# Second attention of a two-layer transformer block: probabilities and operands split and transposed in another way

## The reference, cut to what matters

```python
def second_attention(x, ctx, Wq, Wk, Wv, Wo, q_norm_w, k_norm_w, pos_ctx, pos_x):
    y = layernorm(x)                                   # per batch 128 x 256
    q = rms_norm(y @ Wq.T, q_norm_w)                   # 16 heads of 128
    kv_in = concatenate([ctx, y], axis=1)              # 256 keys
    k = rms_norm(kv_in @ Wk.T, k_norm_w)               # 4 key heads of 128
    v = kv_in @ Wv.T
    q, k = rope(q, pos_x), rope(k, [pos_ctx, pos_x])   # x*cos + rotate_half(x)*sin
    scores = q @ k.T / sqrt(128)                       # each key head serves 4 query heads
    attn = softmax(scores) @ v
    return attn @ Wo.T                                 # 2048 -> 256
```

## Time and profile before

| | us |
|---|---|
| median of 3 runs (949.36 to 957.8) | 949.4 |
| the profiled execution's own time | 950.05 |
| its span, first to last instruction | 948.3 |
| first to last keys-and-values matmul of the second attention | 311.8 to 820.1 |
| last output addition of the second attention | 864.4 |

### The profile page before, as it was taken

How to read it: one execution, slowest core, us unless ns; L and a number is a source line. 1 busy time by engine, 2 the same in 40 slices (tenths; PEclk the granted TensorE clock), 3 DMA queues, 4 the chain that set the end, 5 groups by cost and what they waited for, 6 DMA issues and landing times.

```text
span 948.3 us, 19290 instructions
## 1 busy us (share of the span) xinstructions
PE 786.5 (83%) x5555; PEld 525.6 (55%) x5555; DVE 817.4 (86%) x2370; ACT 599.3 (63%) x1452; POOL 597.1 (63%) x987
## 2 busy tenths in 40 slices
PE   0185989884675679999999999999999999984776
PEld 0152333331233457777777777777777777653433
DVE  7765789976895689999999999999999999954996
ACT  1565787762894267666667766666677766662552
POOL 1500111122573699999999999999999999841453
PEclk9995999997996899999999999999999999998997
DMA  8204355441254000000000000000000000000245
GB/s 302 100 1 135 110 159 158 148 132 49 55 96 94 24 23 7 29 9 22 30 28 2 29 29 23 8 29 30 2 29 29 29 1 13 12 12 12 43 101 120
DMA packets 89306, 53.72 MB, mean 57 GB/s; under 512 B 43988, under 2 KB 88438, under 8 KB 88950
## 3 DMA queue, kind: packets, MB, share of 16 engines
q1 hardware_dynamic: 89206, 52.54, 19.5%
HBM read 22.10 MB, written 6.29 MB: 30 GB/s over the span
## 4 chain that ended last, share of the span: by engine, by line
PE 59%; DVE 13%; issue 10%; POOL 7%; ACT 5%; DMA 3%; SPq 1%; POOLq 1%; DVEq 0%; ACTq 0%
PE psum L1590 8%; PE psum L1614 8%; PE psum L1558 8%; PE psum L1602 8%; PE psum L1545 7%; PE psum L1570 3%; PE psum L1580 3%; PE psum L515 3%; PE psum L1511 2%; DMA arena<-arena 2%; PE psum L501 2%; ACT arena L812 1%; ACT arena L806 1%; PE psum L1530 1%; DVE arena L830 1%
## 5 line engine op out<-in xcount | busy, mean ns | idle before, releaser
L1302 ACT ACTIVATE arena<-psum,arena 128x256 f32<-128x256 f32 x256 | 147.0, 589 | 2.8 <-DVE arena L1495 2.8
L1286 POOL TENSOR_SCALAR arena<-arena 128x256 f32<-128x256 f32 x256 | 123.4, 482 | 35.4 <-DVE arena L1456 13.0
L1311 ACT ACTIVATE arena<-psum 128x512 f16<-128x512 f32 x64 | 38.2, 597 | 158.8 <-PE psum L1614 158.8
L1558 PE MATMUL psum<-wq_t,arena 128*128 128x512 f16 x384 | 94.5, 383 | 4.5 <-DVE arena L1385 4.3
L1590 PE MATMUL psum<-wo_t,arena 128*128 128x256 f16 x768 | 94.4, 273 | 3.0 <-DVE arena L1396 3.0
L1602 PE MATMUL psum<-arena 128*128 128x256 f16 x768 | 94.3, 273 | 2.7 <-ACT arena L1302 2.7
L1545 PE MATMUL psum<-wkv_t,arena 128*128 128x256 f16 x768 | 95.6, 275 | 0.9 <-DVE arena L1422 0.9
L1614 PE MATMUL psum<-arena 128*128 128x512 f16 x384 | 93.3, 379 | 0.0
L1243 POOL TENSOR_TENSOR arena<-arena,minus_half 128x6 f32<-128x6 f32 x64 | 85.1, 1329 | 10.7 <-DVE arena L1487 6.9
L1251 POOL TENSOR_TENSOR arena<-arena 128x256 f32<-128x256 f32 x128 | 90.4, 727 | 0.3 <-DVE arena L1385 0.3
L343 POOL TENSOR_TENSOR arena<-arena 128x256 f32<-128x256 f32 x16 | 11.9, 745 | 116.9 <-DVE arena L422 116.9
(11 more groups left out here) (201 smaller groups left out, 2011.2 us busy)
## 6 DMA issues: line engine op xcount, KB each, us to landing
arena<-split_scratch SPq DMA_DIRECT2D x96, 64.0 KB, 2.6
arena<-in_x SPq DMA_DIRECT2D x32, 128.0 KB, 2.2
split_scratch<-arena SPq DMA_DIRECT2D x32, 128.0 KB, 1.8
x_rows<-arena SPq DMA_DIRECT2D x32, 128.0 KB, 2.0
arena<-x_rows SPq DMA_DIRECT2D x32, 128.0 KB, 2.1
arena<-in_L_ffn_w SPq DMA_DIRECT2D x2, 1024.0 KB, 6.8
x_rows<-in_L_xattn_Wq SPq DMA_DIRECT2D x1, 2048.0 KB, 13.3
ctx_t<-in_L_xattn_Wo SPq DMA_DIRECT2D x1, 2048.0 KB, 11.7
```

The lines of the kernel that those rows point to most:

```text
L1286: eng.tensor_scalar(probs[:, t, h, :], probs[:, t, h, :], share[:, t, h:h + 1], P_SCALE, ALU.mult, ALU.mult).then_inc(S["probs"], 1)
L1302: eng.activation(probs[:, t, h, :], S_BANKS[:, h, :], ACT.Exp, bias=bias[:, t, h:h + 1], scale=r[:, w.lane % 4, h:h + 1], accum_out=total[ ...
L1558: mm = eng.matmul(Q_BANK, y_t[:, p, s, k, :], c.wq_t[:, m, k, SHARE * P * g:SHARE * P * g + SHARE * P], start=(n == 0), stop=(n == 5))
```

## The change

The second attention is written anew, still with 64 units and one list per engine. The lags are now: rows 1, halves of y 2, transpose of y 3, projection 3, transpose of queries and keys 5, scores 6, high halves of the probabilities (PROBS) 7, low halves (LOWS) 8, values 9, output 10.

- No transpose is left on TensorE. SP issues three transposing DMAs per unit: 12 blocks for queries and keys, 8 for the high and 8 for the low halves of the probabilities. Each batch has one more, of 4 blocks, for `y`.
- Exponentials are written back into the score banks in PSUM, which are doubled. ACT makes the high halves from there with the scale `share`, DVE the low halves.
- Sums of squares come from ACT's Square with accumulation, and the inverse roots from its Ln and Exp in place of GpSimd's `pow`.
- DVE forms cosine and sine products in one instruction for the queries and one for each of the two key blocks.
- GpSimd adds the rotated parts, and makes the high and low halves of `y`, queries and keys. It no longer touches the probabilities.
- Rows, context and tables are read where they lie, with no copying DMA.

The diff, cut to its core (`unit(s, LAG)` is the unit of that stage in step s, or None; `batch` the same for the first unit of a batch):

```diff
-            for h in heads:
-                eng.activation(probs[:, t, h, :], S_BANKS[:, h, :], ACT.Exp, bias=bias[:, t, h:h + 1],
-                               scale=r[:, w.lane % 4, h:h + 1], accum_out=total[:, t, h:h + 1])\
-                   .then_inc(S["exps"], 1)
...
+    ROWS, HALVES, Y_TURN, PROJ, QK_TURN, SCORE, PROBS, LOWS, ATTEND, OUT = 1, 2, 3, 4, 5, 6, 7, 8, 9, 10
...
     def sync(eng):
+        def probs_turn(u, half):
+            eng.dma_start_transpose(p_t[:, u % 2, half, :, :, :].rearrange("p h k r -> p (h k) r"),
+                                    p_hl[:, u % 2, half, :, :].rearrange("p h k -> p (h k)"))\
+               .then_inc(p_turned[u % 2], 16)
+        for s in range(STEPS):
+            u = unit(s, LOWS)
+            if u is not None:
+                eng.wait_ge(S["p_lo"], u + 1)
+                probs_turn(u, 1)
+            u = unit(s, QK_TURN)
+            if u is not None:
+                eng.wait_ge(S["q_lo"], u + 1)
+                wait(eng, S["scores"], u - 1)
+                eng.dma_start_transpose(qk_t[:, u % 2, :, :], qk_hl[:, u % 2, :]).then_inc(qk_turned[u % 2], 16)
+            b = batch(s, Y_TURN)
+            if b is not None:
+                eng.wait_ge(S["y_lo"], b + 1)
+                wait(eng, S["q"], GROUPS * (b - 1))
+                eng.dma_start_transpose(y_t[:, b % 2, :, :, :].rearrange("p s k r -> p (s k) r"),
+                                        y_hl[:, :, :].rearrange("p s n -> p (s n)")).then_inc(y_turned[b % 2], 16)
+            u = unit(s, PROBS)
+            if u is not None:
+                eng.wait_ge(S["p_hi"], u + 1)
+                wait(eng, S["attn"], u - 1)
+                probs_turn(u, 0)
     def pool(eng):
...
+        for s in range(STEPS):
+            u = unit(s, PROJ)
+            if u is not None:
+                eng.wait_ge(S["k_cs"], u + 1)
+                wait(eng, S["k_lo"], u)
+                eng.tensor_tensor(straight(k_rot[:, :, :]), straight(k_cs[:, 0, :, :]), swapped(k_cs[:, 1, :, :]),
+                                  ALU.add).then_inc(S["k_rot"], 1)
...
+                wait(eng, qk_turned[u % 2], 16 * (u // 2))
+                eng.tensor_copy(k_hl(u, 0), flat(k_rot[:, :, :])).then_inc(S["k_hi"], 1)
...
+                eng.tensor_tensor(k_hl(u, 1), flat(k_rot[:, :, :]), k_hl(u, 0), ALU.subtract).then_inc(S["k_lo"], 1)
...
+            if u is not None:
+                eng.wait_ge(S["q_cs"], u + 1)
+                wait(eng, S["q_lo"], u)
+                eng.tensor_tensor(straight(q_rot[:, :, :]), straight(q_cs[:, 0, :, :]), swapped(q_cs[:, 1, :, :]),
...
+                eng.tensor_copy(q_hl(u, 0), flat(q_rot[:, :, :])).then_inc(S["q_hi"], 1)
...
+                eng.tensor_tensor(q_hl(u, 1), flat(q_rot[:, :, :]), q_hl(u, 0), ALU.subtract).then_inc(S["q_lo"], 1)
     def scalar(eng):
...
+        for s in range(STEPS):
+            u = unit(s, PROJ)
+            if u is not None:
+                eng.wait_ge(S["kv"], u + 1)
+                wait(eng, S["ss_k"], u)
+                wait(eng, S["r"], 2 * (u - 1))
                 for n in range(2):
+                    last = eng.activation(junk[:, SHARE + n, :], kv_view[:, n, 0, :], ACT.Square,
+                                          accum_out=sums[:, u % 2, SHARE + n:SHARE + n + 1])
+                last.then_inc(S["ss_k"], 1)
...
+                eng.activation(v[:, u % 8, 0, :, :], kv_view[:, :, 1, :], ACT.Copy).then_inc(S["v_hi"], 1)
+            u = s - PROJ
+            if 0 <= u <= TOTAL:
+                cols = slice(0 if u else SHARE, SHARE + 2 if u < TOTAL else SHARE)
+                eng.wait_ge(S["ss_k"], min(u + 1, TOTAL))
+                wait(eng, S["ss_q"], u)
+                wait(eng, S["r"], 2 * u)
+                eng.activation(log_ms[:, cols], sums[:, u % 2, cols], ACT.Ln, scale=1.0 / HEAD_DIM, bias=eps[:, 1:2])\
+                   .then_inc(S["r"], 1)
...
+                eng.activation(r[:, u % 8, cols], log_ms[:, cols], ACT.Exp, scale=-0.5).then_inc(S["r"], 1)
+            u = unit(s, PROBS)
+            if u is not None:
+                eng.wait_ge(S["share"], 2 * (u + 1))
+                eng.wait_ge(S["exps"], u + 1)
+                wait(eng, p_turned[u % 2], 32 * (u // 2))
+                for h in range(SHARE):
+                    last = eng.activation(p_hl[:, u % 2, 0, h, :], s_banks(u)[:, h, :], ACT.Copy,
+                                          scale=share[:, u % 2, h:h + 1])
+                last.then_inc(S["p_hi"], 1)
...
+            u = unit(s, PROJ)
+            if u is not None:
+                wait(eng, S["ss_q"], u)
+                wait(eng, S["r"], 2 * u)
+                eng.wait_ge(S["q_cs"], u + 1)
+                for h in range(SHARE):
+                    last = eng.activation(junk[:, h, :], Q_BANK[:, P * h:P * h + P], ACT.Square,
+                                          accum_out=sums[:, (u + 1) % 2, h:h + 1])
+                last.then_inc(S["ss_q"], 1)
+            u = unit(s, ATTEND)
+            if u is not None:
+                eng.wait_ge(S["attn"], u + 1)
+                wait(eng, S["o"], u - 1)
+                eng.activation(a_t[:, u % 2, 0, :], A_BANK, ACT.Copy, scale=A_SCALE).then_inc(S["a_hi"], 1)
+            u = unit(s, SCORE)
...
+                eng.wait_ge(S["bias"], u + 1)
...
+                for h in range(SHARE):
+                    last = eng.activation(s_banks(u)[:, h, :], s_banks(u)[:, h, :], ACT.Exp,
+                                          bias=bias[:, u % 2, h:h + 1], scale=r_q(u)[:, h:h + 1],
+                                          accum_out=total[:, u % 2, h:h + 1])
+                last.then_inc(S["exps"], 1)
     def vector(eng):
+        for s in range(STEPS + 1):
+            u = unit(s, LOWS)
+            if u is not None:
+                eng.wait_ge(S["p_hi"], u + 1)
+                for h in range(SHARE):
+                    last = eng.scalar_tensor_tensor(p_hl[:, u % 2, 1, h, :], s_banks(u)[:, h, :],
+                                                    share[:, u % 2, h:h + 1], p_hl[:, u % 2, 0, h, :],
+                                                    ALU.mult, ALU.subtract)
+                last.then_inc(S["p_lo"], 1)
...
+            if u is not None:
+                eng.wait_ge(S["a_hi"], u + 1)
+                eng.scalar_tensor_tensor(a_t[:, u % 2, 1, :], A_BANK, A_SCALE, a_t[:, u % 2, 0, :], ALU.mult,
+                                         ALU.subtract).then_inc(S["a_lo"], 1)
+            u = unit(s, PROBS)
+            if u is not None:
+                eng.wait_ge(S["exps"], u + 1)
+                eng.tensor_scalar(part[:, u % 2, :], total[:, u % 2, :], 1.0 / P_SCALE, None, ALU.mult)\
+                   .then_inc(S["share"], 1)
...
+            if u is not None:
+                eng.wait_ge(S["share"], 2 * u + 1)
+                eng.reciprocal(share[:, u % 2, :], part[:, u % 2, :]).then_inc(S["share"], 1)
...
+            u = unit(s, PROJ)
+            if u is not None:
+                bu = u // GROUPS
+                eng.wait_ge(S["r"], 2 * (u + 1))
+                eng.wait_ge(S["v_hi"], u + 1)
+                eng.wait_ge(S["tables"], bu + 1)
+                wait(eng, S["k_rot"], u)
+                for n in range(2):
+                    last = eng.scalar_tensor_tensor(
+                        k_cs[:, :, n, :], kv_view[:, n, 0, :].unsqueeze(1).broadcast_to([P, 2, HEAD_DIM]), r_k(u, n),
+                        turn["k"][:, bu % 2, :, n, :], ALU.mult, ALU.mult)
+                last.then_inc(S["k_cs"], 1)
+                eng.tensor_tensor(v[:, u % 8, 1, :, :], kv_view[:, :, 1, :], v[:, u % 8, 0, :, :], ALU.subtract)\
+                   .then_inc(S["v_lo"], 1)
...
+            if u is not None:
+                eng.wait_ge(S["q"], u + 1)
+                wait(eng, S["q_rot"], u)
+                eng.tensor_tensor(
+                    q_cs[:, :, :, :],
+                    Q_BANK.rearrange("p (h d) -> p h d", h=SHARE).unsqueeze(1).broadcast_to([P, 2, SHARE, HEAD_DIM]),
+                    turn["q"][:, bu % 2, :, :].unsqueeze(2).broadcast_to([P, 2, SHARE, HEAD_DIM]), ALU.mult)\
+                   .then_inc(S["q_cs"], 1)
+            b = batch(s, ROWS)
+            if b is not None:
+                eng.wait_ge(S["rstd"], 2 * (b + 1))
+                wait(eng, S["y_lo"], b)
+                eng.tensor_scalar(y[:, :], c.x_rows[:, b, :], mv[:, 0:1], rstd[:, :], ALU.subtract, ALU.mult)\
                    .then_inc(S["y"], 1)
+            u = unit(s, SCORE)
+            if u is not None:
+                eng.wait_ge(S["scores"], u + 1)
+                wait(eng, S["bias"], u - 1)
+                eng.tensor_reduce(top[:, u % 2, :], s_banks(u), AX.X, ALU.max).then_inc(S["top"], 1)
...
+                eng.scalar_tensor_tensor(bias[:, u % 2, :], top[:, u % 2, :], -1.0, r_q(u), ALU.mult, ALU.mult)\
...
     def tensor(eng):
+        for s in range(STEPS):
+            u = unit(s, PROJ)
+            if u is not None:
```

(46 more changed lines are left out.)

525 lines of the change are left out of this document (111 added, 414 removed).

## The result

The changed kernel takes **927.5 us** (median of 4, 921.53 to 938.8), the kernel before 952.9 beside it: ratio 0.9709, 95% interval 0.9626 to 0.9793. All ratios here compare the means of the fast runs, so this one leaves the run of 938.8 out as a slow one. The forecast was 995 with a chance of 0.19 for a time under 940, so it was wrong in sign. Where a stretch from the start is needed I take e7's profile, a kernel whose batches last as long (32.1 us).

What follows compares the result with a forecast made beforehand. TensorE was taken to set the pace at 8.22 us a step, ScalarE afterwards at 7.57. From 950.05: +56 (late `y`'s 92 included), -8 and -2 give 996, less 0.6 for the median 995 us; 8 in 10 range 930 to 1050.

Steps and rivals of the forecast that it cites:

- SP issues that transpose in the same step, third in its list: Each batch's first projection step: `y`'s transpose queues behind low halves, queries and keys, so the keys come late.
- a late `y`: Keys of the new rows wait for transposed `y`: 6.6 us a batch in 14 batches, 92 us.
- Rival A: SP's wait for the low halves ends some 6 us sooner, so `y` is not late: 903 us, chance 0.12.
- The ring: Waits between ScalarE and VectorE within one second-attention step, from key squares to exponentials, set the pace: 7.57 us.
- 0.24 us to spare: VectorE's maximum and bias run beside ScalarE's query squares and high half (1.73 us) and end 0.24 us sooner.
- beside the rest: GpSimd's new work, 6.2 us a step, lies beside the other engines' work as long as a step is longer.
- Two thirds of TensorE's saving is lost: Second attention: ScalarE becomes the pace, a batch takes 30.6 us against 32.9; TensorE alone would save 107 us.
- B: TensorE stays the pace at 6.55 us a step, ScalarE's waits hidden, `y` late: 934 us, chance 0.06.
- C: ScalarE's squares and copies at their lower ends, 7.0 us a step: 961 us, down to 944, chance 0.12.
- E: ScalarE's Square, Ln, Exp and Copy would reload the tables; nearly excluded, chance 0.01.
- D: Half clock through scores and values after each gap, or dearer squares: 1037 us and above, chance 0.14.
- a sign of error: Heads of the batches: no idle TensorE there would show the forecast wrong; it expected 6 us or more idle.

Runs made afterwards that it cites:

- e7: The changed kernel with SP issuing the transpose of `y` at the head of its step's list; 925.62 us.
- e1: The changed kernel with the transpose of `y` issued one step later, in the step of its own projection; 1030.61 us.
- e12: e2 with one query square instead of four (the other sums a constant) and the maximum over half of the keys; 900.03 us.
- e11: e2 with the maximum of the scores taken over half of the keys only; 909.5 us.
- e10: e2 with one query square instead of four on ScalarE, the three sums left out being a constant; 910.07 us.
- e2: The changed kernel with GpSimd's tables instruction moved behind the queries' halves; 907.72 us.
- e3: The changed kernel with the bias formed head by head, by four VectorE operations with one SBUF tensor and a pointer each; 918.31 us.
- e13: e12 with the bias formed head by head as in e3; 893.73 us.
- e9: e2 with the third pass left out of the queries' and output projections, 0.98 us a step less TensorE work; 910.15 us.

## Why the prediction was wrong

**The step that failed: "SP issues that transpose in the same step, third in its list".** The list of lags has ten names and ten numbers; the transpose of `y` is 3 and the projection is 4. I paired the projection with 3, the value that it had before, and the text on the change says so too ("projection 3"); the line of the diff is right. The transpose stands one step earlier in SP's list than its projection in TensorE's. In the window shown it is issued at 602.19, as TensorE comes to that projection; the matmuls on `y` run from 605.59 to 606.42, and ScalarE, still busy with squares and exponentials, wants the keys only at 607.48. In e1 it is issued at 544.47, when ScalarE has been done for 2 us. The 92 us of a late `y`, the largest correction in the sum, were charged to a wait that the change does not have. Rival A, "`y` is not late", was the true case; I named another place for it (SP's wait for the low halves), and gave it 0.12.

**What a late `y` would cost: nearly right.** I said 6.6 us a batch, half clock included; in e1 ScalarE's wait for the keys alone is 6.6, 15 times and not 14, and a batch lasts 39.2 us instead of 32.0, so 7.2. A transpose of 4 blocks landed after 2.9 us (median), where I had 2.6 and a plain copy of that size 2.1; the rows' figure was nearer than a plain copy's.

**The ring: its length right, its closing incomplete.** The step from 591.61 to 599.10, term by term, predicted and measured: key squares 0.62 and 0.50, high half of the values 0.28 and 0.26, Ln and Exp 0.45 and 0.60, three products on VectorE 2.33 and 2.46, query squares 1.24 and 1.01, high half of the attention 0.49 and 0.48, exponentials 2.16 and 2.18. Sum 7.57 and 7.49. The exponential keeps its pitch of 0.54 whether it is written to PSUM or, before, to SBUF; the Trainium skill, ScalarE: Activation LUTs, Step-by-step: what each stage is for, has PSUM as the faster destination, which shows here in the mean duration alone (541 ns against 589), not in the pitch, and so not in the time.

Behind the query products the step has two branches, squares and high half on ScalarE, maximum and bias on VectorE. I gave the second 0.24 us to spare, from a bias of 0.24. In the step above it has none: the bias ends at 596.89, the exponentials begin at 596.92. Part of that is GpSimd again, in the step that counts as undisturbed:

```profile
596.47 0.40 POOL L1278 CAST arena<-arena 128x256 f16<-128x256 f32 x1
596.48 0.41 DVE L1438 SCALAR_TENSOR_TENSOR arena<-arena 128x4 f32<-128x4 f32 x1
```

At the 0.25 us that it takes in e12's short step the bias would have had 0.16 us to spare. e11 shows the one side: a shorter maximum gains nothing where ScalarE's branch ends last. e10 shows the other, with up to 0.35 us of its bias (0.60 for 0.25) due to the hold. Both together gain 0.7 us in the one step where nothing else holds (7.52 in e2, 6.79 in e12).

**What I did not see: GpSimd holds the bias.** I put GpSimd's new work "beside the rest", as long as its sum is shorter than a step. Its sum was (21.84 of 32.00 us), but an instruction of VectorE with two SBUF inputs waits for GpSimd's running one. The Trainium skill, SBUF — State Buffer, Who interferes with whom, states this: such an instruction contends with a GpSimd instruction that reads SBUF, and one with at most one SBUF input does not, its 2-port modes aside; e3's two lines agree (163 to 1293 ns, against 201 to 216). Measured against the forecast's ring, the hold cost 32.0 - 30.6 = 1.4 us a batch, 21 us in 15 batches; e2 alone gives 1.2 a batch and 20 us back.

**The ledger.** From e7's profile (matmuls on `y`, output additions; ns min/median/max, first and last start), the answer to the earlier trace rows:

```profile
L1457 PE MATMUL psum<-wkv_t,arena x384: 272/273/421, 309.8 to 803.0; 128*128 128x256 f16 x192
```

```profile
L1387 DVE SCALAR_TENSOR_TENSOR x_rows<-psum,x_rows x16: 417/419/425, 384.1 to 838.7; 128x256 f32<-128x256 f32 x16
```

- Up to the first product: 311.8 before, 309.8 now, -2 (predicted 0, within 1). The two points differ a little: 311.8 is the start of all twelve matmuls, 309.8 that of the six on `y`, while the six on the context ran at 303.8 and TensorE then waited for `y`. With half of the 2.74 us for twelve as an estimate, the start on `y` before is 313.2, and the first two parts are -3 and -14.
- First to last product: 508.3 before, 493.2 now, -15. Predicted 564; without the late `y` 472, and the 21 us more are the held bias.
- Last product to last addition: 44.3 before, 35.7 now, -8.6 (predicted 36).
- From there to the end of the span: 83.9 before, 80.7 now, -3 (predicted -2 for the copy).

Together -29, the spans' 948.3 and 919.4. So the gain is 15 us in the steady part and 14 around it. Of the 107 us that TensorE's saving would be worth alone, the ring takes 65 (64 x 1.02), the scaling of the rows 5 and GpSimd's hold 22, which leaves the 15. The first two are the forecast's prices and the third is the rest, so this is a sum that closes by construction; the scaling, priced at 0.3 us a batch, measured 0.41 in e2 (7.93 for 7.52) and 0.67 in e13. "Two thirds of TensorE's saving is lost" stood for the ring; with the hold it is six sevenths.

**The other rivals.** B's 934 is near the result by accident: its mechanism, TensorE as the pace, is excluded by e9 (in e2's kernel). C falls with the terms above: the squares are cheaper by 0.35 us a step, but Ln and Exp and VectorE's products dearer by 0.28. E, reloaded tables, falls with no such idle time on ScalarE. Of D the mechanism exists, at a small price: in the changed kernel TensorE's clock falls behind 6 of the 15 waits for `y` (granted clock 0.50 from 445 to 450 and 0.66 from 638 to 643, against 1.00 from 606 to 611), and of these only the one at 444.85 lengthened its batch, to 33.5 us. In e7, without the wait, the clock stands at 1.00 from 330 to 820 us. Why waits of 2.26 and 2.28 us, at 605.59 and 637.59, differ in this is open. What I had listed as a sign of error came true: no idle TensorE that ScalarE notices at the heads of the batches.

## What to carry to other kernels

Before a wait is priced, write down for producer and consumer the step in which each is issued, from the list of lags itself, name by name; one position was worth 103 us here and turned the sign. When a ring over two engines is priced, follow every branch between its fork and its meeting, since the slack of the shorter one is all that a shortening of the longer one can gain. Where GpSimd gets long instructions on SBUF, look which of VectorE's on the critical path read two SBUF tensors, and move or reshape either.

## What was not expected of the hardware

- A VectorE instruction of 4 columns with two SBUF inputs lasted up to 1293 ns, ending with a GpSimd addition of 1265. GpSimd's total busy time (21.84 of 32.00 us) says nothing of this.
- One SBUF input was no protection for every form. The scaling of the row sums (4 columns, a constant) lasted 0.17 us alone, and in e13 1.10 beside a GpSimd subtraction that began 0.01 us sooner. The form with a pointer on one column was never stretched (201 to 216 ns in e3). The two forms differ in columns and in the kind of scalar, and no run separates these, so the cause is not shown. That row and its neighbour in e13:

```profile
600.00 1.09 POOL L1277 TENSOR_TENSOR arena<-arena 128x512 f16<-128x512 f32 x1
600.01 1.10 DVE L1383 TENSOR_SCALAR arena<-arena 128x4 f32<-128x4 f32 x1 [0.20 <-ACT psum L1359]
```
